# Layer 0's output projection turned round: integer weights stationary in two passes, a turned sum, and probabilities divided before they are used

## The reference

```python
def _dequant_matmul(x, qw, scales):                       # GS = 128, ZERO = 8
    w = (qw.astype(jnp.float32) - ZERO) * jnp.repeat(scales, GS, axis=0)
    return x @ w
...
scores = jnp.einsum('bhqd,bhkd->bhqk', q, k) / math.sqrt(HD)    # 32 heads, 8 kv heads, HD = 128
scores = jnp.where(causal[None, None], scores, jnp.finfo(scores.dtype).min)
attn = jax.nn.softmax(scores.astype(jnp.float32), axis=-1)
ctx = jnp.einsum('bhqk,bhkd->bhqd', attn, v)
ctx = ctx.transpose(0, 2, 1, 3).reshape(b, s, NH * HD)
return _dequant_matmul(ctx, qw_o, scales_o)
...
x = x + ga * _L0_attn_ref(h, ...)                         # ga: one number per output column
```

## Time and profile before

| | |
|---|---|
| median of 3 runs | 1863.04 us (1862.41 to 1863.96) |
| the profiled execution, own time | 1862.15 us |
| its span, first to last instruction | 1860.4 us |
| mean granted TensorE clock | 0.962 |
| busy: PE, DVE, ACT, POOL | 92%, 62%, 43%, 48% |
| heads of layer 0's attention | from 74 us to 1024 us of the span |
| one head there (two successive units 6) | 30.2 us with a turn of v |

### The profile page before, as it was taken

One profiled execution on the slowest core, in us unless ns is written; L12 is line 12 of the kernel. 1 busy time (PEld: TensorE's weight loads), 2 busy tenths in 40 slices (PEclk: granted clock), 3 DMA queues, 4 the chain that ended last, 5 costly groups with the idle time before them and its releaser, 6 DMA issues. The chain is left out here.

```text
span 1860.4 us, 24749 instructions
## 1 busy us (share of the span) xinstructions
PE 1719.2 (92%) x8775; PEld 1256.2 (68%) x8775; DVE 1162.7 (62%) x2505; ACT 808.0 (43%) x1780; POOL 886.6 (48%) x786
## 2 busy tenths in 40 slices
PE   5699999999999999999999599998849999999778
PEld 3477777777777777777776388876735555554557
DVE  6866666666666666666655823345787766774475
ACT  3345454555545454554544211100315666666221
POOL 1587697786877968769673400000352222211200
PEclk9799999999999999999999799999879999999889
DMA  6111101010010101010100321103100000000021
GB/s 188 35 35 29 35 18 46 18 46 29 23 46 18 46 18 35 24 34 18 35 12 1 117 68 52 30 1 126 54 0 1 1 1 1 1 1 1 29 44 46
DMA packets 75315, 63.36 MB, mean 34 GB/s; under 512 B 23470, under 2 KB 53358, under 8 KB 75194
## 3 DMA queue, kind: packets, MB, share of 16 engines
q1 hardware_dynamic: 75194, 61.79, 11.0%
HBM read 59.68 MB, written 2.10 MB: 33 GB/s over the span
## 5 line engine op out<-in xcount | busy, mean ns | idle before, releaser
L844 ACT ACTIVATE a_probs<-psum,a_neg_max 128x128 f32<-128x128 f32 (+7 forms) x256 | 190.1, 743 | 240.4 <-DVE a_neg_max L768 240.0
L768 DVE CUSTOM_DVE_ANT_0 psum<-psum,a_keys_allowed 128x128 f32<-128x128 f32 (+7 forms) x256 | 195.1, 762 | 110.3 <-PE psum L77 110.1
L698 PE MATMUL psum<-a_probsT,a_v 128*128 128x512 f32 (+3 forms) x768 | 258.4, 486 | 0.2 <-ACT a_probsT L855 0.2
L698 PEld LDWEIGHTS psum<-a_probsT,a_v 128*128 128x128 f32 x768 | 144.6, 190 | 117.3 <-issue 91.8
L1715 ACT ACTIVATE a_probsT<-psum 128x512 f32<-128x512 f32 (+3 forms) x384 | 172.4, 495 | 84.7 <-PE psum L1553 62.3
L780 DVE SCALAR_TENSOR_TENSOR x<-psum,a_row_inv,x 128x512 f32<-128x512 f32 x256 | 191.0, 748 | 16.9 <-PE psum L77 11.2
L785 DVE TENSOR_TENSOR a_ctxT_lo<-psum,a_ctxT_hi 128x512 fp32r<-128x512 f32 x64 | 44.3, 692 | 216.0 <-ACT a_ctxT_hi L861 216.0
L855 ACT COPY a_probsT<-psum 128x512 f32<-128x512 f32 (+3 forms) x384 | 170.9, 484 | 9.9 <-PE psum L685 9.8
L685 PE MATMUL psum<-ident,a_probs 128*128 128x128 f32 x1152 | 171.7, 273 | 0.4 <-ACT a_probsT L855 0.4
L685 PEld LDWEIGHTS psum<-ident,a_probs 128*128 128x128 f32 x1152 | 138.7, 140 | 32.6 <-DVE x L780 4.7
L558 POOL TENSOR_TENSOR a_turned_pool<-a_q_sum,a_sine 64x512 f32<-64x512 f32 x62 | 79.8, 1288 | 167.3 <-DVE a_q_sum L754 166.2
(11 more groups left out here) (302 smaller groups left out, 4122.3 us busy)
## 6 DMA issues: line engine op xcount, KB each, us to landing
a_raw_q<-in_L_attn_qw_q SPq DMA_DIRECT2D x32, 256.0 KB, 4.0
a_raw_o<-in_L_attn_qw_o SPq DMA_DIRECT2D x32, 256.0 KB, 2.6
a_raw_scale_o<-in_L_attn_scales_o SPq DMA_DIRECT2D x32, 256.0 KB, 3.6
mod1b_w<-in_L_wmod SPq DMA_DIRECT2D x4, 1024.0 KB, 11.4
mod0a_w<-in_L_wmod SPq DMA_DIRECT2D x3, 1024.0 KB, 10.8
mod0b_w<-in_L_wmod SPq DMA_DIRECT2D x3, 1024.0 KB, 7.4
f_raw<-in_L_ffn_down_w SPq DMA_DIRECT2D x10, 256.0 KB, 3.1
f_raw<-in_L_ffn_gate_w SPq DMA_DIRECT2D x10, 256.0 KB, 3.3
```

Source lines behind the costliest of these rows:

```text
L698: last = nc.tensor.matmul(bank(use)[:, first:HALF], v[:, g % 2, j, :], probsT[b][:, j, first:HALF], start=(j == 0), stop=(j == keys - 1))
L768: nc.vector.tensor_tensor_reduce(out=scores, in0=scores, in1=keys_allowed[:, S - (i + 1) * P:S], scale=-1.0, scalar=-MASKED, op0=ALU.add, ...
L844: nc.scalar.activation(probs[:, u % 3, 0:(i + 1) * P], score[u % 2][:, 0:(i + 1) * P], ACT.Exp, bias=neg_max[:, h % 2, i:i + 1], scale=-1. ...
```

## The change

1. **Output projection turned.** The integer weights of a head (minus 8) are exact in one part, so they stand still in PE as the left operand, and the high and low parts of the values stream past: two passes instead of three. The result has output columns on partitions and queries along the row. A head's eight products are four column tiles for each half of the queries, where there were eight query tiles.
2. **Scales.** Each product is multiplied by its scale times the gate, one number per partition (`scale_o`), and added by DVE to a new tile `sumT` [128 x 4 x 1024]. `make_o` on POOL goes, with its four instructions a head; the conversion on ACT stays and writes `wo` itself.
3. **Division.** DVE no longer has a query row per partition there, so the probabilities are divided before they are turned: DVE makes the inverse sum of every unit ([128 x 1], 256 instructions in place of 32 of [128 x 8]) and ACT multiplies the unit's probabilities by it in SBUF (`weigh`, 256 new instructions of 128 to 1024 columns). The transposes wait for `weighed` in place of `exped`.
4. **End.** After the last head `sumT` is turned back by PE (32 transposes) and added to `x` by DVE (8 instructions).
5. **Start.** The scale rows [32 x 512] are loaded once, multiplied by the gate on POOL, turned by PE and copied by ACT; POOL clears `sumT`.
6. **Loads.** The broadcast scale loads (256 KB a head) go; `raw_q` and `raw_o` have one buffer in place of two, so each of their loads waits for the conversion before it.

```diff
-    uses += [("o", LAST_HEAD, t) for t in range(TPH)] + [("pv", LAST_HEAD, 1)] + [("o", LAST_HEAD, t) for t in range(TPH, NT)]
+    first_half, second_half = range(TPH), range(TPH, NT)
+    uses += [("o", LAST_HEAD, n) for n in first_half] + [("pv", LAST_HEAD, 1)] + [("x", t) for t in first_half]
+    uses += [("o", LAST_HEAD, n) for n in second_half] + [("x", t) for t in second_half]
...
         def load_q(sp, h):
-            if h >= 2:
-                sp.wait_ge(*wq_made.of(h - 2))
+            if h:
+                sp.wait_ge(*wq_made.of(h - 1))
...
         def load_o(sp, h):
-            if h >= 2:
-                sp.wait_ge(*o_shifted.of(h - 2))
-                sp.wait_ge(*o_made.of((h - 2, "scale")))
-            sp.dma_start(raw_o[:, h % 2, :], qw["o"][h * HD0:(h + 1) * HD0, :]).then_inc(o_in[h % 2], 16)
-            sp.dma_start(raw_scale_o[:, h % 2, :], scales["o"][h:h + 1, :].broadcast_to([P, D])).then_inc(o_in[h % 2], 16)
+            if h:
+                sp.wait_ge(*wo_made.of(h - 1))
+            sp.dma_start(raw_o[:, :], qw["o"][h * HD0:(h + 1) * HD0, :]).then_inc(o_in, 16)
...
+        def make_wo(act, h):
+            act.wait_ge(o_in, 16 * (h + 1))
+            if h >= 2:
+                act.wait_ge(*filled.of(("o", h - 2, NT - 1)))
+            nc.scalar.activation(wo[:, h % 2, :], raw_o[:, :], ACT.Copy, bias=-ZERO_POINT).then_inc(wo_made.sem, 1)
...
+            pool.wait_ge(tables_in, 64)
+            pool.tensor_tensor(scale_rows_o, scale_rows_o, mem.gate[0:NH0, 0, :], ALU.mult).then_inc(drawn.sem, 1)
+            pool.memset(sumT[:, :, :], 0.0).then_inc(drawn.sem, 1)
+            pool.wait_ge(*drawn.of("sum"))
             turn(("k", 0, 0))
             turn(("k", 0, 1))
             for h in HEADS:
                 if h > 0:
                     turn(("q", h, 1))
-                make_o(h)
...
             def turn_probs(u):
 
                 h, i = units[u]
-                pe.wait_ge(*exped.of((h, i)))
+                pe.wait_ge(*weighed.of((h, i)))
...
-            def output(h, t):
-                use = ("o", h, t)
-                if t % TPH == 0:
-                    pe.wait_ge(*ctx_lo.of((h, t // TPH)))
-                if t == 0:
-                    pe.wait_ge(*o_made.of((h, "lo")))
+            def output(h, n):
+
+                (b, j), use = divmod(n, KT), ("o", h, n)
+                if j == 0:
+                    pe.wait_ge(*ctx_lo.of((h, b)))
+                if n == 0:
+                    pe.wait_ge(*wo_made.of(h))
                 wait_bank(use)
-                split_products(nc.tensor, bank(use)[:, :], [part[:, tile(t)] for part in ctxT],
-                               [part[:, h % 2, :] for part in wo], True, True).then_inc(filled.sem, 1)
+                w = wo[:, h % 2, tile(j)]
+                nc.tensor.matmul(bank(use)[:, :], w, ctxT[1][:, half(b)], start=True, stop=False)
+                nc.tensor.matmul(bank(use)[:, :], w, ctxT[0][:, half(b)], start=False, stop=True).then_inc(filled.sem, 1)
...
+            def turn_sum(t):
+
+                use = ("x", t)
+                pe.wait_ge(*added.of((LAST_HEAD, t // TPH * KT + KT - 1)))
+                wait_bank(use)
+                for j in kts:
+                    last = nc.tensor.transpose(bank(use)[:, tile(j)], sumT[:, j, tile(t)], mem.ident[:, :])
+                last.then_inc(filled.sem, 1)
...
-            def invert(h):
-                dve.wait_ge(*exped.of((h, NT - 1)))
-                nc.vector.reciprocal(row_inv[:, h % 2, :], row_sum[:, h % 2, :]).then_inc(inverted.sem, 1)
-                dve.wait_ge(*inverted.of(h))
-
-            def add_output(h, t):
-                use = ("o", h, t)
+            def invert(u):
+                h, i = units[u]
+                dve.wait_ge(*exped.of((h, i)))
+                nc.vector.reciprocal(row_inv[:, h % 2, i:i + 1], row_sum[:, h % 2, i:i + 1]).then_inc(inverted.sem, 1)
+
+            def add_output(h, n):
+
+                (b, j), use = divmod(n, KT), ("o", h, n)
+                total = sumT[:, j, half(b)]
                 dve.wait_ge(*filled.of(use))
...
-                nc.vector.scalar_tensor_tensor(out=mem.x[:, t, :], in0=bank(use)[:, :], scalar=row_inv[:, h % 2, t:t + 1],
-                                               in1=mem.x[:, t, :], op0=ALU.mult, op1=ALU.add).then_inc(added.sem, 1)
+                nc.vector.scalar_tensor_tensor(out=total, in0=bank(use)[:, :], scalar=scale_o[:, j, h:h + 1], in1=total,
+                                               op0=ALU.mult, op1=ALU.add).then_inc(added.sem, 1)
+
+            def finish(t):
+                dve.wait_ge(*filled.of(("x", t)))
+                nc.vector.tensor_tensor(mem.x[:, t, :], mem.x[:, t, :], bank(("x", t))[:, :], ALU.add
+                                        ).then_inc(finished.sem, 1)
...
             for u, (h, i) in enumerate(units):
                 if u + 1 < len(units):
                     maximum(u + 1)
+                invert(u)
                 if h > 0:
-                    if i == 0:
-                        invert(h - 1)
                     add_output(h - 1, i)
...
+            def weigh(u):
+
+                h, i = units[u]
+                act.wait_ge(*inverted.of((h, i)))
+                row = probs[:, u % 3, 0:(i + 1) * P]
+                nc.scalar.activation(row, row, ACT.Copy, scale=row_inv[:, h % 2, i:i + 1]).then_inc(weighed.sem, 1)
...
                 if u + 1 < len(units):
                     exponential(u + 1)
+                weigh(u)
```

More of the change, by code:

```diff
@@ L389, in layer0_attention_phase @@
     partials = [(key, k) for key in FIRST_KEYS for k in kts]
-    uses = [("part", key, k) for key, k in partials] + [("vt", 0, b) for b in halves]
+    uses = [("part", key, k) for key, k in partials] + [("vt", 0, b) for b in halves] + [("so",)]
     for u, (h, i) in enumerate(units):
@@ L572, in _ @@
         def _(sp):
+            sp.dma_start(scale_rows_o, scales["o"]).then_inc(tables_in, 16)
+            load_q(sp, 1)
             load_kv(sp, "k", 1)
@@ L577, in _ @@
                     load_kv(sp, "k", g + 2)
+                if h + 1 <= LAST_HEAD:
+                    load_o(sp, h + 1)
                 if h + 2 <= LAST_HEAD:
@@ L626, in taken_out @@
                     return added.of(name)
+                if kind == "x":
+                    return finished.of(*name)
+                if kind == "so":
+                    return scales_made.of("o")
                 if kind == "pv":
@@ L739, in _ @@
             turn_probs(len(units) - 1)
-            for t in range(TPH):
-                output(LAST_HEAD, t)
+            for n in first_half:
+                output(LAST_HEAD, n)
             values(LAST_HEAD, 1)
-            for t in range(TPH, NT):
-                output(LAST_HEAD, t)
+            for t in first_half:
+                turn_sum(t)
+            for n in second_half:
+                output(LAST_HEAD, n)
+            for t in second_half:
+                turn_sum(t)
         @block.vector
@@ L812, in _ @@
                     split_values(*values_due(h, i))
-            invert(LAST_HEAD)
-            for t in range(TPH):
-                add_output(LAST_HEAD, t)
+            for n in first_half:
+                add_output(LAST_HEAD, n)
             split_values(LAST_HEAD, 1)
-            for t in range(TPH, NT):
-                add_output(LAST_HEAD, t)
+            for t in first_half:
+                finish(t)
+            for n in second_half:
+                add_output(LAST_HEAD, n)
+            for t in second_half:
+                finish(t)
         @block.scalar
@@ L833, in take_first @@
                                      ).then_inc(first_out.sem, 1)
-            def shift_o(h):
-                act.wait_ge(o_in[h % 2], 32 * (h // 2 + 1))
-                if h:
-                    act.wait_ge(*o_made.of((h - 1, "scale")))
-                nc.scalar.activation(shifted[:, :], raw_o[:, h % 2, :], ACT.Copy, bias=-ZERO_POINT).then_inc(o_shifted.sem, 1)
             def exponential(u):
@@ L873, in _ @@
             make_wkv(act, "k", 1)
-            shift_o(0)
+            make_wo(act, 0)
+            act.wait_ge(*filled.of(("so",)))
+            nc.scalar.copy(scale_o[:, :, :].rearrange("p k h -> p (k h)"), bank(("so",))[:, 0:KT * NH0]
+                           ).then_inc(scales_made.sem, 1)
             exponential(0)
```

84 lines of the change are left out of this document (40 added, 44 removed).

## The result

| | before | changed |
|---|---|---|
| median | 1862.72 us (4 runs, 1860.63 to 1863.96) | 1882.37 us (4 runs, 1881.90 to 1885.35) |
| ratio, 95% interval | | 1.0115 [1.0102, 1.0127] |
| profiled execution, own time and span | 1862.15, 1860.4 us | 1882.72, 1880.8 us |

What follows compares the result with a forecast made beforehand. PE was taken to bound the stage, its saving counting only where ACT's chain keeps up. Heads 1 to 27 +3, others +2.5, +2.5, +1.5, end +4.5, start +0.5 made +14.5 us: 1877 us, range 1849 to 1893.

Steps and rivals of the forecast that it cites:

- the promise: Output projection on PE: 8 passes fewer a head at 0.23 us each, 1.84 us a head, 59 us over 32 heads.
- Price of a multiplication: ACT's `weigh`: steps of 0.87 us at 896 columns, 0.98 at 1024, 0.66 at 640, 0.23 at 128; bounds 0.1 both ways.
- The integer row: Profile row of an ACT conversion with integer source in SBUF, 0.642 us, taken to show an SBUF source costs nothing extra.
- Stretch one: Unit 2 to unit 6 of a head: PE saves 0.92 us, loses 0.5 waiting for ACT's copy, keeps 0.4.
- Stretch two: Unit 6 to the long product (values, second half of queries): product starts at 11.5 to 11.6 us, on the mean 0.45 later.
- Head 0 and heads 28 to 30: Head 0 saves no passes, +2.5 us; heads 28 to 30, without k or v quarters, +0.8 each, +2.5 us.
- Last head: ACT's chain before the last head's last product: +1.5 us.
- The end: Last high part to last sum: 5.2 us before, 9.8 us now with DVE's twelve instructions and PE's transposes, +4.5 us.
- The start: Before head 0: POOL's clearing and scaling nearly all hidden; four small transposes, a copy and the first multiplication, +0.5 us.
- The signs: Heads 29.9 to 30.5 us; PE waits 1.9, busy near 94%, clock 1.00; ACT +180 us, POOL -150; end 9.8.
- The saving arrives: Rival: ring and probability buffers absorb unevenness, unit 7's turned probabilities out by 10.4 us after unit 6; 1811 us, chance 0.08.
- The clock: Rival: PE's short waits lower the mean clock of the 940 us to 0.95, 50 us more, 1925 us; chance 0.05.

Runs made afterwards that it cites:

- e3: The kernel before with two passes in the output projection in place of three, nothing else; 1814.51 us (ratio to before 0.9742).
- e1: The changed kernel without ACT's multiplication of the probabilities, DVE still making all 256 inverses; 1825.26 us (ratio to before 0.9799).
- e5: The changed kernel with each multiplication moved behind ACT's copies of the turned probabilities; 1862.65 us (ratio to before 1.0001).
- e10: The changed kernel with multiplications of units 0 to 5 behind the copies and both weight conversions at unit 1; 1846.24 us (ratio to before 0.9919).

## Why the prediction was right

The place, the mechanism and the sign were right, and so was the time within its range. Of its terms those for the heads were too small by 7.0 us together and the one for the end by 0.9; the start was 2.1 us less than said, which took some of that back by luck.

**What bounds.** Right: PE had no slack to lose and ACT's order decided. e3 shows the promise (48 us of the 59 worked out), e1 that the multiplication takes it back.

**Price of a multiplication.** Slightly low. Groups by shape, 100 to 1000 us, in the changed kernel (busy, mean ns), beside the earlier trace rows:

```profile
L884 ACT ACTIVATE a_probs<-a_probs,a_row_inv 128x1024 f32<-128x1024 f32 x30 | 34.9, 1162 | 0.0
...
L884 ACT ACTIVATE a_probs<-a_probs,a_row_inv 128x896 f32<-128x896 f32 x30 | 31.0, 1033 | 0.0
...
L884 ACT ACTIVATE a_probs<-a_probs,a_row_inv 128x512 f32<-128x512 f32 x30 | 21.4, 713 | 0.0
L875 ACT ACTIVATE a_probs<-psum,a_neg_max 128x512 f32<-128x512 f32 x30 | 20.7, 690 | 37.6 <-DVE a_neg_max L791 37.6
...
L884 ACT ACTIVATE a_probs<-a_probs,a_row_inv 128x128 f32<-128x128 f32 x30 | 13.0, 434 | 0.0
```

Steps to the next start at 896, 1024, 640 and 128 columns were 0.94, 1.04, 0.72 and 0.29 us where 0.87, 0.98, 0.66 and 0.23 were taken: 0.06 more each, well inside the bounds of 0.1. At 512 columns a source in SBUF is dearer than the same columns from PSUM by 0.02 us (0.713 against 0.690 for the exponential and 0.697 for the scaled copy); at 128 columns the multiplication lasts 0.06 more than the exponential. The integer row that I followed gave nothing. The Trainium skill ("VectorE: DVE Perf Modes", section on the TRN2 errata) has ScalarE's fixed part as 224 cycles from SBUF against 172 from PSUM, which makes 0.04 us as an estimate: the sign agrees, and against the scaled copy of 512 columns this trace has half of that. Its five microseconds would have made the forecast 1882, but the place where they would have come from, the row of ACT, took only 0.04 us more than said, so that agreement is chance.

**Stretch one.** Right: wait and restart cost 0.48 us (5.34 for the unit against 4.86 in e5) where 0.5 was said, and the gain left was 0.44 (13.27 to 12.83) where 0.4 was said.

**Stretch two.** Right in place and size: ACT ends 11.54 us in, said 11.5. Two small errors nearly cancel in that: the three multiplications take 2.27 us and not 2.08, the rest of the row 6.27 and not 6.4. The product then starts at 11.67 to 11.75, said 11.5 to 11.6, in all heads with quarters of k or v, so those with a turn of v, which PE had set, lost 0.4 us and those without 0.8. The mean loss is 0.6 and not 0.45, which over 27 heads makes the +6.0 in place of +3. The term that was too small is the 0.45, since PE starts the product 0.15 to 0.2 us behind the copies.

**Head 0 and heads 28 to 30.** +2.5 against 3.2, and +2.5 against 4.1. In head 0 some 0.4 us come from a load of ACT's table, 1.28 us: before, it lay hidden at 63.27; now it begins at 72.24, behind the new copy of the scales, and the first exponential waits for it. In heads 28 and 29 the long product came 9.73 us after unit 6 before, not the 9.9 that I worked out, and 11.1 now, not 10.9; in head 30 it went from 8.81 to 10.52. Each head lost 1.4 to 1.7 us in stretch two, and not 1.0.

**Last head.** Mis-sized: "+1.5" against 3.2. PE and then ACT there:

```profile
1021.61 1.02 PE L683 MATMUL psum<-ident,a_probs 128*128 128x128 f32 x7 [1.98 <-ACT a_probs L884]
1023.40 1.97 PE L683 MATMUL psum<-ident,a_probs 128*128 128x128 f32 x8 [0.77 <-ACT a_probs L884]
```
```profile
1020.52 1.03 ACT L884 ACTIVATE a_probs<-a_probs,a_row_inv 128x896 f32<-128x896 f32 x1
...
1022.18 1.17 ACT L884 ACTIVATE a_probs<-a_probs,a_row_inv 128x1024 f32<-128x1024 f32 x1
```

No scores of a next head stand between the turnings, so both multiplications lie bare: PE waits 1.98 and 0.77 us, where before it waited 0.39 once, and the mean clock is 0.79 from 1020 to 1025. I had counted ACT's chain there and not PE's loss of cover.

**The end.** 10.6 us, said 9.8; without the fall of the clock it is 9.56 (e10). So the count of DVE's instructions held.

**The start.** Said +0.5, came -1.6. PE's first 16 modulation matmuls lasted 8.55 us in place of 9.94 with the same instructions: they follow one another at steps of 0.85 us first and of 0.43 later, and the changed kernel has three or four of the long steps where the kernel before has six or seven. The trace's first record of the clock, full speed, stands where the steps shorten: at 18.75 us before and at 15.96 now. Over the runs here the start of head 0 lies between 71.9 and 74.2 without order, so the -1.6 says nothing of the change. POOL's clearing and scaling stayed hidden.

**The signs.** Heads of 30.2 us, the clock and POOL's 151 us less came as said; ACT is busier by 157 and not 180. PE was to be busy 94% in the stage and to wait 1.9 us a head; it is busy 97.3% and idle 0.8. Yet a head has eight passes fewer and is 0.2 us longer, so some 2 us a head are lost. Busy time shows less than half of them, since a matmul behind a wait also lasts longer (0.50 in place of 0.40 in the rows at 536 us).

**The rivals.** The saving arrives: e1 shows that its condition was right (10.11 us to ACT's copy, under 10.4), and its 28.3 us a head came without the multiplication only. The clock did not fall in the stage: with three to five short waits a head it stands at 1.00 from 400 to 600 us. The rule that I had cited ("TensorE: Matmul & The Clock Gate" in the Trainium skill, PSUM-queue depth-cycling) does not bite here. From head 0 on the clock falls only near the end of the phase, after PE's waits of 1.98 and 0.77 us and after the one of 1.91, and the latter in four executions of eight.

## What to carry to other kernels

Before costing a saving on the bound engine, follow the queue of the engine that must keep up with it through one period, in order: what it costs is set by where a new instruction stands between a wait and its follower, not by its share of busy time. Then try moving work before removing it: here the same instructions in another order were worth 36 us. And check a new order for loops: an instruction moved behind a copy that needs another engine's answer turns two queues into one.

## What was not expected of the hardware

- The halves of the change did not add: -48 and +30 gave +20, since each hid part of the other.
- Sixteen small transposes took 3.49 or 1.97 us in the same code, by the granted clock alone (0.66 or 1.00), behind a wait of the same 1.91 us. Of the eight profiled executions with this end four have 1.97 us and four 2.74 to 3.49. A kernel that ends in such a tail has up to one microsecond that nothing in its code explains.
